# Moving one small sum and its ReLU behind the last head's maxima on VectorE, and one GpSimd multiply ahead of another

## The reference, cut to what matters

```
x = x + cross_attention(layernorm(x), ctx)      # 16 heads, 2048 keys a head
x = x + retention(layernorm(x))                 # 8 heads, 128 rows
x = x + fff_block(layernorm(x))                 # four trees: q, k, v and f
```

```
leaf = walk(x)                                       # argmax over 256 paths
h    = relu(einsum('bsd,bsdl->bsl', x, w1[leaf]) + b1[leaf])   # "up" rows, 16 wide
out  = einsum('bsl,bsld->bsd', h, w2[leaf]) + b2[leaf]          # "down" rows
```

## Time and profile before

| | |
|---|---|
| three runs | 650.86, 651.43, 654.0 us; median 651.43 us |
| span of the profiled execution | 648.7 us, 11000 instructions |
| the profiled execution's own time | not given beside its span; the median lies 2.7 us above the span |
| busy: TensorE / VectorE / ScalarE / GpSimd | 615.9 (95%) / 460.2 (71%) / 393.2 (61%) / 263.8 (41%) us |
| mean granted clock of TensorE | 0.997 of full speed |
| chain that ended last, by engine | TensorE 65%, GpSimd 13%, VectorE 9%, DMA 5%, ScalarE 4%, issue 3% |

### The profile page before, as it was taken

One profiled execution on the slowest core, in us unless ns is written; L12 is line 12 of the kernel. 1 busy time (PEld: TensorE's weight loads), 2 busy tenths in 40 slices (PEclk: granted clock), 3 DMA queues, 4 the chain that ended last, 5 costly groups with the idle time before them and its releaser, 6 DMA issues.

```text
span 648.7 us, 11000 instructions
## 1 busy us (share of the span) xinstructions
PE 615.9 (95%) x4235; PEld 536.6 (83%) x4235; DVE 460.2 (71%) x816; ACT 393.2 (61%) x834; POOL 263.8 (41%) x252
## 2 busy tenths in 40 slices
PE   7899999999999999998999999998999999888887
PEld 4688888999898989878898989877898989885674
DVE  3666656778778677878776777877777777875853
ACT  4665566576656555786655865777554855742571
POOL 2210000230202102997525155997343247974533
PEclk9899999999999999999999999999999999999999
DMA  9910000010100004440030016240030008021933
GB/s 199 239 34 2 0 1 1 1 52 16 66 1 1 2 1 145 191 133 1 1 135 2 1 50 255 100 134 2 1 135 1 2 5 330 5 70 57 352 133 138
DMA packets 21402, 48.54 MB, mean 75 GB/s; under 512 B 1508, under 2 KB 14696, under 8 KB 17256
## 3 DMA queue, kind: packets, MB, share of 16 engines
q0 software_dynamic: 4608, 34.74, 14.4%
q1 hardware_dynamic: 16168, 12.85, 7.4%
q10 hardware_dynamic: 576, 0.26, 0.1%
HBM read 47.59 MB, written 0.26 MB: 74 GB/s over the span
## 4 chain that ended last, share of the span: by engine, by line
PE 65%; POOL 13%; DVE 9%; DMA 5%; ACT 4%; issue 3%; SPq 1%; POOLq 0%; DVEq 0%; ACTq 0%
PE ps_s L466 22%; PE ps_av L466 21%; PE ps_ring L741 14%; POOL leaf L1575 4%; PE ps_m L466 4%; PE ps_ring L466 4%; POOL leaf L1579 2%; DMA leaf<-wk_t_dram 2%; DVE chunk_max L1426 2%; DMA w_room<-down_k_dram,idx 2%; ACT prob L1084 2%; DVE pt_lo L1169 2%; POOL ct_lo L1544 2%; ACT pt_hi L1015 1%; DMA leaf<-down_f_dram,idx 1%
## 5 line engine op out<-in xcount | busy, mean ns | idle before, releaser
L1015 ACT CAST pt_hi<-ps_ring 128x512 fp32r<-128x512 f32 x256 | 144.5, 590 | 154.4 <-PE ps_ring L741 154.2
L1169 DVE TENSOR_TENSOR pt_lo<-ps_ring,pt_hi 128x512 fp32r<-128x512 f32 x256 | 170.3, 686 | 58.8 <-ACT pt_hi L1015 58.7
L1084 ACT ACTIVATE prob<-ps_s,neg_max 128x1024 f32<-128x1024 f32 x128 | 141.6, 1113 | 22.9 <-DVE neg_max L1509 22.8
L741 PE MATMUL ps_ring<-ident,prob 128*128 128x128 f32 x1024 | 145.1, 274 | 9.4 <-DVE x_sb L1458 4.1
L466 PE MATMUL ps_av<-pt_hi,c_hi 128*128 128x256 f32 x512 | 151.3, 295 | 1.2 <-issue 1.2
L1426 DVE TENSOR_REDUCE chunk_max<-ps_s 128x1 f32<-128x1024 f32 x128 | 150.5, 1216 | 1.9 <-PE ps_s L466 1.7
L741 PEld LDWEIGHTS ps_ring<-ident,prob 128*128 128x128 f32 x1024 | 117.8, 141 | 35.8 <-issue 23.6
L466 PE MATMUL ps_av<-pt_lo,c_hi 128*128 128x256 f32 x512 | 144.7, 283 | 0.0
L466 PE MATMUL ps_av<-pt_hi,c_lo 128*128 128x256 f32 x512 | 144.7, 283 | 0.0
L466 PE MATMUL ps_s<-ct_hi,q_hi 128*128 128x512 f32 x256 | 112.4, 439 | 3.9 <-POOL ct_lo L1544 1.3
L466 PE MATMUL ps_s<-ct_hi,q_lo 128*128 128x512 f32 x256 | 101.3, 396 | 0.0
(11 more groups left out here) (293 smaller groups left out, 759.6 us busy)
## 6 DMA issues: line engine op xcount, KB each, us to landing
stage<-ctx_t_dram SPq DMA_DIRECT2D x16, 256.0 KB, 3.8
stage<-ctx_rows_dram SPq DMA_DIRECT2D x16, 256.0 KB, 3.1
leaf<-w_v_dram SPq DMA_DIRECT2D x1, 512.0 KB, 9.1
leaf<-w_o_dram SPq DMA_DIRECT2D x1, 512.0 KB, 11.2
dec<-decay_dram SPq DMA_DIRECT2D x1, 512.0 KB
nw<-node_w_dram SPq DMA_DIRECT2D x1, 510.0 KB
wsm<-w_small_dram SPq DMA_DIRECT2D x1, 448.0 KB
leaf<-wq_t_dram SPq DMA_DIRECT2D x1, 384.0 KB, 11.4
```

Source lines behind the costliest of these rows:

```text
L741: last = nc.tensor.transpose(o[:, i * P:(i + 1) * P], prob[:, n % 2, k:k + P], ident[:])
L1015: nc.scalar.copy(pt_hi[:, pp, row:row + KPC, P * (n % 2):P * (n % 2 + 1)], ps_ring[:, i % 2, :].rearrange("p (k q) -> p k q", k=KPC)).then ...
L1084: nc.scalar.activation(prob[:, n % 2, 1024 * e:1024 * (e + 1)], ps_s[:, 1024 * e:1024 * (e + 1)], ACT.Exp, bias=neg_max[:, n:n + 1], accum ...
L1169: return nc.vector.tensor_tensor(o, a, b_, op)
```

## The change

For batch 2 alone, the sum `hid1` of the second tree moves on VectorE from u = 62 (ahead of the maxima of head 63) to u = 63 (behind them, behind the last two `lower` calls of slot 63 and behind `weights`). Its ReLU moves from GpSimd to VectorE, directly behind the sum. On GpSimd `up2` moves from u = 63 to 62 and `weigh1` from u = 62 to 63. GpSimd's order for batch 2 was up1, weigh0, relu1, weigh1, up2, gather_down2, fold0 and is now up1, weigh0, up2, gather_down2, weigh1, fold0.

```
     ("PE", "third_sum"): 90,
+    ("DVE", "hid1"): 63,
     ("DVE", "hid2"): 1000,
...
     ("Pool", "gather_down2"): 63,
-    ("Pool", "up2"): 63,
+    ("Pool", "up2"): 62,
+    ("Pool", "weigh1"): 63,
...
                     if t:
                         nc.vector.reduce_sum(hid[:, t, :], w, axis=AXX).then_inc(S["hid_ready"], 1)
+                        if (b, t) == (B - 2, 1):
+                            dve.wait_ge(S["hid_ready"], 3 * b + 1)
+                            nc.vector.tensor_scalar_max(hid[:, t, :], hid[:, t, :], 0.0).then_inc(S["relu_done"], 1)
                         return
...
                 elif k[:4] == "relu":
-                    if b < B - 1 and k != "relu0":
+                    if b < B - 1 and k != "relu0" and (b, k) != (B - 2, "relu1"):
                         relu(b, int(k[4]))
```

## The result

The changed kernel took 653.94 us in the median of 18 runs (651.88 to 657.1), the kernel before 650.9 us in 18 runs beside it (648.15 to 654.0). The ratio is 1.0047 with a 95% interval of 1.0033 to 1.0061: 3.1 us slower (2.1 to 4.0), just inside the 0.5% within which the forecast called it no change. 652.8 us was forecast. The profiled execution took 656.0 us, 2.1 us over the median, with a span of 654.2 us, against a span of 648.7 us before, and a mean granted clock of TensorE of 0.984 against 0.997.

A forecast was written before the change was run, and what follows sets the result against it. `add_output` of X63 on VectorE was taken to set T(62,1) and the drain to the end; 2.10 us taken from ahead of the maxima against the late sum and held ReLU gave +1.34, so 651.43 + 1.34 = 652.8 us, range 650.3 to 654.9.

The forecast's parts named there:

- The main case: VectorE's new ReLU is held by GpSimd's multiply without a fall of TensorE's clock: +1.34 us, 652.8 us, chance 0.70.
- the rival that had a chance of 0.10: TensorE's clock falls after standing 3.2 us ahead of T(62,1): up to +1.7 us on top, 654.5 us, chance 0.10.
- What bounds the drain's start: `add_output` of X63 on VectorE sets T(62,1) on TensorE, which starts 0.15 us behind it.
- What the change takes away: On VectorE a 0.88 us wait and a 1.22 us sum leave from ahead of head 63's maxima: 2.10 us sooner there.
- The held ReLU: VectorE's ReLU waits for GpSimd's third-tree multiply, 2.17 us from 563.83 to 566.00, so T(62,1) starts 1.34 us later.
- nothing holds the ReLU: Rival: VectorE's ReLU ends at 564.0 and T(62,1) starts at 564.92: -0.64 us, 650.8 us, chance 0.10.
- One to one to the end: A shift of T(62,1) on TensorE shifts the end of the kernel by the same amount.
- GpSimd and ScalarE at nothing: GpSimd's new order and ScalarE's later `down1` blocks cost nothing; GpSimd has 3.41 us of slack ahead of 582.84.
- The clock: TensorE's clock falls to 1.2 GHz after standing 3.2 us, slowing T(62,1) and what follows: up to +1.7 us, chance 0.10.
- has busy time on both sides: Argument against a fall of the clock: TensorE is busy before and after its 3.2 us of standing ahead of T(62,1).
- The sum: The whole kernel: 651.43 + 1.34 = 652.8 us, or by the span 648.7 + 1.34 = 650.0 us.

The follow-up runs named there:

- the PSUM variant: The changed kernel with the second tree's sum written to PSUM and its ReLU reading it there; 649.38 us, ratio 0.9974 to the kernel before.
- the best order: As the PSUM variant, with the second tree's sum and ReLU moved behind `add_output` of X63 on VectorE; 648.86 us, ratio 0.9981 to the kernel before.
- the last PSUM variant: As the best order, with the first tree's sum of batches 0 to 2 also written to PSUM for its ReLU; 649.34 us, ratio 0.9978.

## Why the prediction was right, and where it was not

The time lies in the stated range, and the way down to the start of T(62,1) is confirmed step by step. The main case is not: it said 1.34 us more with the full clock, and 3.1 us more were measured, most of the difference by the rival that had a chance of 0.10. That 653.94 still looks close to 652.8 is in part luck, as the forecast set out from a median of three runs (651.43) that lay 0.5 us above that of 18 (650.9), and "no change" held by 0.03% only.

- *What bounds the drain's start.* Shown. T(62,1) waits for `add_output` of X63; the profile of the changed kernel names it, and moving the sum behind it brought T(62,1) to 4.49 us behind `weigh0`.
- *What the change takes away.* Shown: the maxima of head 63 start at 558.73 against 560.59, on a timeline that is 0.24 us later as a whole, so 2.10 us sooner; X63 waits no more.
- *The held ReLU.* Right in mechanism: 2.29 us against 2.17 us forecast, its end 0.03 us behind the multiply's. The size of the step was 1.34 us and T(62,1) came 1.16 us later (7.35 - 6.19). The 0.18 us are in the addition of durations: `add_output`'s first record starts at 566.08, ahead of the recorded end of the ReLU (566.17), where I had put one record behind the other, and the multiply took 4.55 us. The same addition had the rival "nothing holds the ReLU" at -0.64 us; the PSUM variant shows -0.93 (5.26 - 6.19).
- *One to one to the end.* Shown for the drain: 1.19 us at its end with the clock kept (22.39 - 21.20). The run times agree, with 1.2 us by the medians, but their interval reaches from -1.0 to +2.0 us.
- *GpSimd and ScalarE at nothing.* Right here. `weigh1` started 0.01 us behind `gather_down2`, and GpSimd's idle time ahead of the root grew from 3.41 to 6.96 us.
- *The clock.* Right as a mechanism, wrong in its chance. The step that failed is the sentence that the hole "has busy time on both sides", with a chance of 0.10: with the mechanism given 3.2 us of hole, which came out as 3.30 us, the fall came in three profiles of three. Its price, up to 1.7 us, measured 1.06 to 1.97 us. The forecast for this rival, 654.5 us, lies nearer to the measured 653.94 us than the main one. Against the measured 650.9 us before, the same sum (1.34 + 1.7) gives 653.9 us. The page named with this rival, "TensorE: Matmul & The Clock Gate" of the Trainium skill, section "HAM oscillation", has idle gaps between groups of matmuls send the clock back, and the falls behind 3.30 us agree; it doesn't say that a gap of just this length must do it.
- *The sum.* Hold 1.2 us, clock in the drain 1.4 us in the mean of three (1.97, 1.06, 1.13), together 2.6 us of the 3.1 us (2.1 to 4.0). The rest of some 0.5 us is within the interval. Falls behind the drain were in all three profiles of the changed kernel and in one of three of before, and that part was 1.2 us longer in their means (69.5 against 68.2 us). The clocks of the single runs, too, leave some 2.7 us at the lower level beyond the mean of 4.5 us in the drain, by the estimate above. Whether the change makes these falls likelier stays open: five of the ten profiles of other kernels have them as well.

## What to carry to other kernels

Before a small one-source VectorE operation between SBUF operands is put on a critical queue, look at what GpSimd runs at that moment: here 16 columns cost 2.29 us behind a long multiply and 0.17 us with the source in PSUM or with GpSimd idle. When a forecast opens a hole on TensorE, price the clock behind it as part of the step and not as an unlikely extra; filler matmuls in the hole tell the two apart. A wait moved away from one place is worth only what the next queue lets through: of the 2.10 us taken from ahead of the maxima the best order kept 1.0 us at the drain's end.

## What the runs showed of the hardware that was not expected

- A wait of TensorE of 2.97 us, at another place of the drain, also brought the lower clock; waits of 0.98, 1.21, 1.23 and 1.25 us ahead of T(62,1) or X63 did not. But a fall needs no such wait: the one at 596.4 us in the first profile of the changed kernel came behind 10 us with no wait over 0.52 us.
- What the lower clock costs behind the drain varies. That part took 67.9 to 68.1 us in the five profiles without a fall, 68.6 us in both with 3.4 us of it, 68.5, 68.9, 69.1, 69.3 and 70.4 us in the five with 6.8 us, and 70.2 us in the one with 10.2 us. All cost less than half of the low stretch's length, and all but the 70.4 us (the last PSUM variant) far less; why that one cost more stays open.
- The hold of VectorE by GpSimd left no trace among the waits: the row shows a long duration, the chain shows "issue", and only the coincidence with the other engine's end gives it away.
